# Convolution, two quantised stages and a dense layer in one kernel: another order in front, the bias row spread by TensorE, the second dense half catching up from four steps behind to two

## The chip, the cores and the metric

One core of a Trainium2 chip. The metric is the device time of one execution in microseconds, here the median of three runs. The profile is of one further execution; its times count from the first instruction.

## What is computed

x has shape (64, 64, 1024). The reference, cut to what matters:

```python
out = lax.conv_general_dilated(x, weight, padding=[(4, 4)], feature_group_count=4)   # 9 taps
out = out + einsum('nd,od->no', cond, c_weight)[:, :, None] + fside[None, :, None]
# _fake_quant(v, bits, axis): scale = max|v| / (2**(bits-1) - 1); round(v / scale) * scale
xq = _fake_quant(out, bits=8, axis=-1)
kq = _fake_quant(kernel, bits=8, axis=0)
y = einsum('bsd,df->bsf', xq, kq) + _fake_quant(bias, bits=16, axis=-1)
return x + _fake_quant(y, bits=8, axis=-1)
```

## The kernel before

The 64 x 64 rows of 1024 are cut into 32 tiles of 128 rows (8 samples, one of 4 groups). Each tile goes through five stages, spread over the engines, and the loops of all engines run over steps k = 0, 1, ...:

- ScalarE rounds x of tile k + 2 to a high part (`round_x`, L265), GpSimd subtracts to get the low part (`split`, L218).
- TensorE convolves tile k: two matmuls with the context (L386) and twelve with the taps (L396), in 512 columns each.
- VectorE takes the column maxima (`column_max`, L564, L572), TensorE spreads them over the rows (`spread_max`, L407), VectorE makes the scales (`levels`, L579 to L590) and rounds one half of the tile to integers (L594), ScalarE the other (`round_levels`, L304). One step later TensorE turns these levels (`turn_levels`, L416) and ScalarE copies them to SBUF as bf16 (`take_levels`, L295).
- TensorE multiplies with the kernel, 8 matmuls of 128x512 (`dense`, L427) for each half of the 1024 outputs: the first half of tile k - 2 and the second half of tile k - 4 in step k (`LAG = (2, 4)`). `dense_ps` has one bank of 512 columns for each half. So `dense(t, h)` waits until `biased{h}` of tile t - 1 is signalled: VectorE has multiplied by the scales (`scale_half`, L550) and added the bias into `y` (`add_bias`, L559).
- VectorE takes the maximum of the row of y (`out_scale`, L604 to L611) for tile k - 5 (`TAIL`), ScalarE converts it to integers and back (`quantise`, L312, L315), GpSimd adds x (`add_x`, L227), and a DMA stores it. The last tile goes in halves (`quantise_last` L323, `add_x_last` L618).

The order of each engine is written out by hand, in one loop per engine; an engine does its instructions in this order, and waits stand ahead of the instruction that needs them. All transfers of x and out are issued by SyncE.

In steps 0 to 4 the kernel matrix is prepared between the tiles: four loads of 1 MB (`load_k`), maxima and scales (`k_levels`, L523 to L534), conversion to integers by VectorE or for two of the eight blocks by ScalarE (`k_round`, L270), turning by TensorE (`k_turn`, L440, L449), copies by ScalarE (`k_take`, L277, L279). The banks of `dense_ps` serve for it. The bias is loaded to all 128 partitions (512 KB, L169), VectorE makes its scale in step 1 (`bias_scale`, L540 to L546), ScalarE its levels in step 2 (`bias_levels`, L285, L288).

Of the kernel before, what the change touches and what calls it, by code (L numbers as in the profile page):

```python
# [28 lines left out]
LAG = (2, 4)  # L29
TAIL = LAG[1] + 1  # L30
XWIN, XSPLIT, LEVELS, YRING, ORING, RSRING = 4, 3, 6, 5, 5, 8
# [8 lines left out]
def build(nc, xw, xr, wt, cond_t, cw_t, cond_bias, ker, bias, out):  # L40
    with ExitStack() as ctx:
# [6 lines left out]
        def sem(name):  # L48
# [26 lines left out]
        b_row = sb("b_row", [P, F], F32)  # L75
        b_stat = sb("b_stat", [P, 4], F32)
        b_int = sb("b_int", [P, F], I16)
# [13 lines left out]
        y_max = sb("y_max", [P, 2], F32)  # L91
        y_scale = sb("y_scale", [P, 2], F32)
# [18 lines left out]
            "b_rounded", "b_made",  # L111
# [3 lines left out]
            "y_max_made", "y_scale_made", "y_inv_made", "y_rounded", "y_dequantised", "o_made", "last_rounded", "last_made")}  # L115
# [15 lines left out]
        def there(t):  # L131
            return 0 <= t < TILES

# [15 lines left out]
        def _(sp):  # L149
# [37 lines left out]

            for k in range(1, TILES + TAIL + 1):
                if XWIN <= k + XWIN - 1 < TILES:
                    load_xwin(k + XWIN - 1)  # L190
                if there(k - TAIL + 2):
                    load_x(k - TAIL + 2)
                if 0 <= k - TAIL - 1 < LAST:
                    store(k - TAIL - 1)
# [6 lines left out]
        def _(pool):  # L201
# [32 lines left out]
            for k in range(TILES + TAIL):  # L234
                if there(k + 2):
                    split(k + 2)
                if 0 <= k - TAIL < LAST:
                    add_x(k - TAIL)

        @block.scalar  # L240
        def _(act):
            act.dma_start(condt[:], cond_t).then_inc(s["cond_in"], 16)
            act.dma_start(cwt[:], cw_t).then_inc(s["cond_in"], 16)
            act.dma_start(cbias[:], cond_bias.unsqueeze(0)).then_inc(s["cond_in"], 16)
            act.wait_ge(s["ones_made"], 1)
# [37 lines left out]
            def bias_levels():  # L283
# [4 lines left out]
                act.activation(bq[:], b_int[:], ACT.Copy, scale=b_stat[:, 1:2]  # L288
                               ).then_inc(s["b_made"], 1)
# [36 lines left out]
            round_x(0)  # L326
            k_round(1)
            k_take(0)
            k_take(1)
            round_x(1)  # L330
            for k in range(TILES + TAIL - 1):
                if k == 2:
# [4 lines left out]
                    bias_levels()  # L337
                elif k == 3:
                    k_take(7)
                    k_take(8)  # L340
                    take_levels(2)
# [8 lines left out]
                if k == 0:  # L350
                    k_round(3)
                    k_take(2)
                    k_take(3)
                    k_take(4)
                if there(k - TAIL):
                    quantise(k - TAIL)
# [5 lines left out]
        def _(pe):  # L362
# [48 lines left out]
            def turn_levels(t):  # L411
                wait(pe, "a_rounded_dve", t + 1)
                wait(pe, "a_rounded", t + 1)
                wait(pe, "a_made", t)
                for j in range(NS):
# [47 lines left out]
            for k in range(TILES + LAG[1]):  # L463
# [6 lines left out]
                if k == 1:  # L470
                    k_turns(2, 4)
                if k == 3:
                    k_turns(7, 8)
                if k in (2, 3, TILES):
                    dense(k - LAG[0], 0)
                    if k == TILES:
                        dense(k - LAG[1], 1)
                    turn_levels(k - 1)
                    if k == 2:
                        k_turns(5, 6)  # L480
                    if there(k):
                        spread_max(k)
                elif k == 1:
# [194 lines left out]
```

## Time and profile before

| what | value |
|---|---|
| median of 3 runs | 280.97 us (279.25 to 282.17) |
| the profiled execution, own time | 278.56 us |
| its span, first to last instruction | 276.7 us |
| mean granted TensorE clock | 0.986 |
| busy, TensorE / VectorE / ScalarE / GpSimd | 251.1 / 238.8 / 185.2 / 153.8 us |

Busy time is the time in which an engine ran an instruction; the granted clock is the share of TensorE's full clock that it was given. Own time is longer than the span by 1.86 us of start and end.

### The profile page before, as it was taken

What the parts mean: (1) busy time and instruction counts of PE and PEld (TensorE: products, weight loads), DVE (VectorE), ACT (ScalarE), POOL (GpSimd) and SP (SyncE); (2) the same over time, 40 slices, a digit from 0 to 9 for tenths busy, and PEclk for the clock granted to TensorE, in tenths of its full rate; (3) what the DMA queues carried; (4) which work ended last, traced back from release to release, by engine and by line L of the source; (5) the groups of instructions that cost most, each with busy time, mean ns of one, the idle gap of its engine ahead of it and who ended that gap; (6) DMA issues with size and microseconds to landing.
All of it is one profiled execution on the core that took longest, in us unless ns stands there. A gap on an engine that the chain in (4) does not pass through costs nothing.

```text
span 276.7 us, 4240 instructions
## 1 busy us (share of the span) xinstructions
PE 251.1 (91%) x1372; PEld 163.5 (59%) x1372; DVE 238.8 (86%) x509; ACT 185.2 (67%) x278; POOL 153.8 (56%) x71
## 2 busy tenths in 40 slices
PE   7866769999999999999999999999999999997540
PEld 3555557666666666666666666666666666663210
DVE  1799964799999999999999999999999989999984
ACT  6257586477777777777777777777777767564762
POOL 2533333356666666666666666666666666533453
PEclk9979999999999999999999999999999999999996
DMA  6997322406666565566666766666666663333355
GB/s 253 416 408 301 123 84 103 153 0 227 223 203 212 211 202 212 203 217 217 209 204 210 230 228 228 228 227 226 219 203 197 218 218 117 144 142 139 107 220 219
DMA packets 15799, 56.04 MB, mean 203 GB/s; under 512 B 1954, under 2 KB 1954, under 8 KB 15778
## 3 DMA queue, kind: packets, MB, share of 16 engines
q1 hardware_dynamic: 15488, 55.71, 56.8%
q8 instruction: 11, 0.18, 0.3%
q10 hardware_dynamic: 290, 0.07, 0.1%
q14 instruction: 10, 0.08, 0.1%
HBM read 38.99 MB, written 16.78 MB: 202 GB/s over the span
## 4 chain that ended last, share of the span: by engine, by line
PE 81%; DVE 8%; ACT 4%; DMA 3%; issue 2%; SPq 0%; DVEq 0%
PE dense_ps L427 36%; PE conv_ps L396 31%; PE turn_ps L416 5%; PE conv_ps L386 5%; DMA k_raw<-ffn_kernel 3%; DVE dense_ps L550 2%; DVE y L559 2%; DVE y_max L604 2%; ACT kq L279 2%; PE small_ps L407 2%; PE dense_ps L449 1%; DVE k_max L523 1%; ACT a_int L304 1%; PE dense_ps L440 1%; ACT x_hi L265 1%
## 5 line engine op out<-in xcount | busy, mean ns | idle before, releaser
L427 PE MATMUL dense_ps<-kq,a_t 128*128 128x512 bf16 x512 | 120.6, 379 | 6.1 <-DVE y L559 5.0
L218 POOL TENSOR_TENSOR x_lo<-xwin,x_hi 128x1032 fp32r<-128x1032 f32 x32 | 76.6, 2393 | 80.8 <-ACT x_hi L265 80.8
L227 POOL TENSOR_TENSOR o_sb<-y,o_sb 128x1024 f32<-128x1024 f32 x31 | 73.9, 2384 | 32.8 <-ACT y L315 32.7
L427 PEld LDWEIGHTS dense_ps<-kq,a_t 128*128 128x128 bf16 x512 | 48.9, 101 | 53.7 <-issue 6.7
L295 ACT CAST a_t<-turn_ps 128x1024 bf16<-128x1024 int16 x32 | 32.4, 1012 | 48.5 <-PE turn_ps L416 48.5
L564 DVE TENSOR_REDUCE small_ps<-conv_ps 128x8 f32<-128x1024 f32 x32 | 39.4, 1232 | 13.8 <-PE conv_ps L396 13.5
L550 DVE SCALAR_TENSOR_TENSOR dense_ps<-dense_ps,row_scale,k_scale_b 128x512 f32<-128x512 f32 x64 | 47.7, 745 | 3.6 <-PE dense_ps L427 3.6
L312 ACT ACTIVATE y_int<-y,y_inv 128x1024 int16<-128x1024 f32 x31 | 35.6, 1148 | 22.3 <-DVE y_inv L611 22.1
L559 DVE TENSOR_TENSOR y<-dense_ps,bq 128x512 f32<-128x512 f32 x64 | 43.9, 685 | 2.8 <-ACT bq L288 1.6
L604 DVE TENSOR_REDUCE y_max<-y 128x1 f32<-128x1024 f32 x32 | 38.7, 1210 | 0.7 <-issue 0.2
L304 ACT ACTIVATE a_int<-conv_ps,inv 128x128 int16<-128x128 f32 x128 | 36.0, 363 | 1.1 <-DVE inv L590 1.1
L315 ACT ACTIVATE y<-y_int,y_scale 128x1024 f32<-128x1024 int16 x31 | 35.7, 1153 | 1.0
L396 PE MATMUL conv_ps<-x_hi,w_hi 128*128 128x512 f32 x128 | 36.2, 405 | 0.0
L265 ACT CAST x_hi<-xwin 128x1032 fp32r<-128x1032 f32 x32 | 33.8, 1055 | 3.0 <-DMA xwin<-x_windows 3.0
L396 PE MATMUL conv_ps<-x_hi,w_lo 128*128 128x512 f32 x128 | 35.5, 399 | 0.0
L396 PE MATMUL conv_ps<-x_lo,w_hi 128*128 128x512 f32 x128 | 35.2, 397 | 0.0
L396 PEld LDWEIGHTS conv_ps<-x_hi,w_lo 128*128 128x128 f32 x128 | 24.4, 191 | 6.2
L396 PEld LDWEIGHTS conv_ps<-x_lo,w_hi 128*128 128x128 f32 x128 | 24.0, 188 | 6.2 <-POOL x_lo L218 0.2
L396 PEld LDWEIGHTS conv_ps<-x_hi,w_hi 128*128 128x128 f32 x128 | 24.7, 193 | 4.8
L386 PE MATMUL conv_ps<-select,ctx 128*128 128x512 f32 x64 | 25.0, 474 | 1.9 <-ACT x_hi L265 1.6
L594 DVE TENSOR_TENSOR a_int<-conv_ps,inv 128x512 int16<-128x512 f32 x32 | 22.1, 691 | 1.1
L416 PE MATMUL turn_ps<-ident_b,a_int 128*128 128x128 bf16 x256 | 19.8, 220 | 1.6 <-ACT a_int L304 1.6
(55 smaller groups left out, 160.2 us busy)
## 6 DMA issues: line engine op xcount, KB each, us to landing
xwin<-x_windows SPq DMA_DIRECT2D x32, 516.0 KB, 4.8
o_sb<-x_rows SPq DMA_DIRECT2D x32, 512.0 KB, 5.3
out<-o_sb SPq DMA_DIRECT2D x31, 512.0 KB, 2.9
k_raw<-ffn_kernel SPq DMA_DIRECT2D x4, 1024.0 KB, 10.5
w_raw<-taps SPq DMA_DIRECT2D x2, 256.0 KB, 3.2
b_row<-ffn_bias SPq DMA_DIRECT2D x1, 512.0 KB, 15.9
out<-o_sb SPq DMA_DIRECT2D x2, 256.0 KB, 2.7
condt<-cond_t ACTq DMA_DIRECT2D x1, 32.0 KB
```

Of the source, the lines that this page charges most:

```text
L218: pool.tensor_tensor(x_lo[:, at].rearrange("p n b -> p (n b)"), xwin[:, t % XWIN, :], x_hi[:, at].bitcast(F32).rearrange("p n b -> p (n b) ...
L227: pool.tensor_tensor(o_sb[:, at, :], y[:, t % YRING, :], o_sb[:, at, :], ALU.add).then_inc(s["o_made"], 1)
L265: act.copy(x_hi[:, t % XSPLIT].rearrange("p n b -> p (n b)"), xwin[:, t % XWIN, :]).then_inc(s["hi_made"], 1)
L304: ins = act.activation(a_int[:, at, n * BLOCKS:(n + 1) * BLOCKS], conv_cols(at)[:, n, :], ACT.Copy, scale=inv8[:, at, n:n + 1])
L315: act.activation(y[:, t % YRING, :], y_int[:, t % 2], ACT.Copy, scale=y_scale[:, t % 2:t % 2 + 1]).then_inc(s["y_dequantised"], 1)
L386: mm = pe.matmul(conv_ps[:, at, hs, :].rearrange("p (n b) -> p n b", n=NH), ctx2[:, g].rearrange("k q o -> k (q o)"), select[:, ns].unsque ...
L396: mm = pe.matmul(conv_ps[:, at, hs, :].rearrange("p (n b) -> p n b", n=NH), w[:, ch, g].rearrange("p q o -> p (q o)"), x[:, x_at, hs * NH: ...
L427: mm = pe.matmul(dense_ps[:, h, :], a_t[:, t % LEVELS, q].rearrange("b j o -> b (j o)"), kq[:, q, half(h)], start=(q == 0), stop=(q == Q - 1))
L550: dve.scalar_tensor_tensor(out=dense_ps[:, h, :], in0=dense_ps[:, h, :], scalar=row_scale[:, t % RSRING:t % RSRING + 1], in1=k_scale_b[:, ...
L559: dve.tensor_tensor(y[:, t % YRING, half(h)], dense_ps[:, h, :], bq[:, half(h)], ALU.add).then_inc(s[f"biased{h}"], 1)
L564: dve.tensor_reduce(cmax_ps, conv_ps[:, t % 2].rearrange("p h (n b) -> p (h n) b", b=BLOCKS), AX_X, ALU.max, apply_absolute_value=True).th ...
L604: dve.tensor_reduce(y_max[:, at], y[:, t % YRING, :], AX_X, ALU.max, apply_absolute_value=True).then_inc(s["y_max_made"], 1)
```

## The change

Four edits:

1. `LATE, CATCH_UP = 4, (12, 20)`: the second half of tile t is done in step t + 4 for t below 12, t + 3 from 12 on, t + 2 from 20 on (`second_step`). Steps 15 and 22 hold two second halves; the first of these stands ahead of the convolution. A tile's maximum, quantisation and store follow one step after its second half (`outs`), so that steps 16 and 23 hold two. There are 35 steps in place of 37. `o_sb` has 6 buffers in place of 5, and the load of x rows for tile t is issued in SyncE's step t + 1 in place of t + 3.
2. The bias is loaded to one partition (4 KB, by ScalarE's queue), its statistics and levels are made there, and two float32 matmuls with a row of ones (`bias_spread`) put it into the bank of `turn_ps`, from where ScalarE copies the halves (`bias_take`).
3. The order in front: bias statistics first, kernel maxima apart from kernel scales, x of tile 1 and tile 2 loaded one kernel pair earlier, some copies and turns in another order.
4. The maximum of the last tile is taken in halves (`maximum_last`, `scale_last`).

The diff, cut:

```diff
-LAG = (2, 4)
-TAIL = LAG[1] + 1
-XWIN, XSPLIT, LEVELS, YRING, ORING, RSRING = 4, 3, 6, 5, 5, 8
+LAG, LATE, CATCH_UP = 2, 4, (12, 20)
+XWIN, XSPLIT, LEVELS, YRING, ORING, RSRING = 4, 3, 6, 5, 6, 8
+        def second_step(t):
+            return t + LATE - sum(t >= t0 for t0 in CATCH_UP)
+        def seconds(k):
+            return [t for t in range(TILES) if second_step(t) == k]
+        def outs(k):
+            return seconds(k - 1)
+        STEPS = second_step(LAST) + 2
...
             load_k(0)
+            load_xwin(1)
             load_k(1)
-            load_xwin(1)
             load_k(2)
+            load_xwin(2)
             load_k(3)
-            load_xwin(2)
-            sp.dma_start(b_row[:], bias.partition_broadcast(P)).then_inc(s["b_in"], 16)
...
             round_x(0)
+            bias_levels()
+            round_x(1)
             k_round(1)
+            bias_take(0)
             k_take(0)
             k_take(1)
-            round_x(1)
-            for k in range(TILES + TAIL - 1):
-                if k == 2:
+            bias_take(1)
+            for k in range(STEPS - 1):
+                if k == 0:
+                    round_x(2)
+                elif k == 1:
+                    take_levels(0)
+                    k_round(3)
+                    k_take(2)
+                    k_take(3)
+                    k_take(4)
+                    round_x(3)
+                elif k == 2:
                     take_levels(1)
                     k_take(5)
                     k_take(6)
                     round_x(4)
-                    bias_levels()
...
+                for t in outs(k):
+                    quantise(t)
...
+            def bias_spread(h):
+                pe.wait_ge(s["b_row_made"], 1)
+                wait(pe, "b_made", h)
+                pe.matmul(turn_ps[:].rearrange("b j p -> b (j p)").bitcast(F32), ones[0:1, :],
+                          bq_row[:, half(h)], start=True, stop=True).then_inc(s["b_spread"], 1)
...
+                if len(again) == 2:
+                    dense(again[0], 1)
                 if there(k):
                     conv(k)
                 if k == 0:
+                    bias_spread(0)
                     k_turns(0, 1)
+                    bias_spread(1)
+                    spread_max(k)
...
+            bias_scale()
+            k_maxima(0)
             k_levels(0)
...
+                for t in outs(k):
+                    if t != LAST:
+                        out_scale(t)
...
+                if k - LAG == LAST:
+                    maximum_last(0)
+                if again:
+                    scale_half(again[-1], 1)
+                    add_bias(again[-1], 1)
+            maximum_last(1)
+            scale_last()
             add_x_last()
```

TensorE's order from the end of step 14 to the convolution of step 15; `biased1` is the signal that the second half's bank has been read out. Before:

```order
L407 MATMUL small_ps<-col_max,same_b 128x64 [waits col_max_masked]
L427 MATMUL dense_ps<-kq,a_t 128x512 [waits biased1,a_made]
L427 MATMUL dense_ps<-kq,a_t 128x512 x7
L386 MATMUL conv_ps<-select,ctx 128x512 [waits hi_made,a_rounded,a_rounded_dve]
L386 MATMUL conv_ps<-select,ctx 128x512
```

Now:

```order
L432 MATMUL small_ps<-col_max,same_b 128x64 [waits col_max_masked]
L454 MATMUL dense_ps<-kq,a_t 128x512 [waits biased1,a_made]
L454 MATMUL dense_ps<-kq,a_t 128x512 x7
L454 MATMUL dense_ps<-kq,a_t 128x512 [waits biased1,a_made]
L454 MATMUL dense_ps<-kq,a_t 128x512 x7
L411 MATMUL conv_ps<-select,ctx 128x512 [waits hi_made,a_rounded,a_rounded_dve]
L411 MATMUL conv_ps<-select,ctx 128x512
```

A second group of eight with the same wait stands between the last half of step 14 and the convolution; the same holds ahead of step 22.

ScalarE's order from step 15's levels to step 16's: `take_levels`, `round_x`, `quantise`, `round_levels`. Before:

```order
L295 CAST a_t<-turn_ps 128x8x8x16
L265 CAST x_hi<-xwin 128x1032
L312 ACTIVATE y_int<-y,y_inv 128x1024
L315 ACTIVATE y<-y_int,y_scale 128x1024
L304 ACTIVATE a_int<-conv_ps,inv 128x128 x4
```

Now:

```order
L314 CAST a_t<-turn_ps 128x8x8x16
L279 CAST x_hi<-xwin 128x1032
L331 ACTIVATE y_int<-y,y_inv 128x1024
L334 ACTIVATE y<-y_int,y_scale 128x1024
L331 ACTIVATE y_int<-y,y_inv 128x1024
L334 ACTIVATE y<-y_int,y_scale 128x1024
L323 ACTIVATE a_int<-conv_ps,inv 128x128 x4
```

The second pair of conversions stands ahead of the levels (L304 is L323 now); the same holds in step 23.

VectorE's order at the end, from the bias add of tile 31's first half on. Before (a bias add, the last maximum with its scale, and L618 follow):

```order
L559 TENSOR_TENSOR y<-dense_ps,bq 128x512
L550 SCALAR_TENSOR_TENSOR dense_ps<-dense_ps,row_scale,k_scale_b 128x512
L559 TENSOR_TENSOR y<-dense_ps,bq 128x512
L604 TENSOR_REDUCE y_max<-y 128x1
L608 TENSOR_SCALAR y_scale<-y_max 128x1
L611 RECIPROCAL y_inv<-y_scale 128x1
L550 SCALAR_TENSOR_TENSOR dense_ps<-dense_ps,row_scale,k_scale_b 128x512
L559 TENSOR_TENSOR y<-dense_ps,bq 128x512
L604 TENSOR_REDUCE y_max<-y 128x1
L608 TENSOR_SCALAR y_scale<-y_max 128x1
L611 RECIPROCAL y_inv<-y_scale 128x1
L550 SCALAR_TENSOR_TENSOR dense_ps<-dense_ps,row_scale,k_scale_b 128x512
```

Now:

```order
L603 TENSOR_TENSOR y<-dense_ps,bq 128x512
L682 TENSOR_REDUCE last_max<-y 128x1
L594 SCALAR_TENSOR_TENSOR dense_ps<-dense_ps,row_scale,k_scale_b 128x512
L603 TENSOR_TENSOR y<-dense_ps,bq 128x512
L682 TENSOR_REDUCE last_max<-y 128x1
L671 TENSOR_REDUCE y_max<-last_max 128x1
L675 TENSOR_SCALAR y_scale<-y_max 128x1
L678 RECIPROCAL y_inv<-y_scale 128x1
L662 SCALAR_TENSOR_TENSOR o_sb<-y_int,y_scale,o_sb 128x512 x2
```

The scale and bias of other tiles' second halves and two maxima are gone from between, and the last maximum is in two halves and a small third.

## Rows read from the trace of the kernel before

**Rows 1.** The page: busy time (us, share, instructions), and the chain by line (shares of the span)

```profile
PE 251.1 (91%) x1372; PEld 163.5 (59%) x1372; DVE 238.8 (86%) x509; ACT 185.2 (67%) x278; POOL 153.8 (56%) x71
...
PE dense_ps L427 36%; PE conv_ps L396 31%; PE turn_ps L416 5%; PE conv_ps L386 5%; DMA k_raw<-ffn_kernel 3%; DVE dense_ps L550 2%; DVE y L559 2%; DVE y_max L604 2%; ACT kq L279 2%; PE small_ps L407 2%; PE dense_ps L449 1%; DVE k_max L523 1%
```

**Rows 2.** Stretches: busy us and instructions by engine, granted clock, DMA share, GB/s

```profile
100.00:150.00 50.00, 50.00 (x270) 32.90 (x268) 46.18 (x105) 37.03 (x56) 32.03 (x15) 1.00 0.64 222
```

**Rows 3.** Timeline, TensorE, steps 30 and 31 (start us, duration us, engine, line)

```profile
235.34 0.78 PE L386 MATMUL conv_ps<-select,ctx 128*128 128x512 f32 x2
...
241.13 1.89 PE L427 MATMUL dense_ps<-kq,a_t 128*128 128x512 bf16 x8
...
242.67 0.78 PE L386 MATMUL conv_ps<-select,ctx 128*128 128x512 f32 x2
```

**Rows 4.** Timeline, the end: VectorE and ScalarE

```profile
260.13 0.69 DVE L559 TENSOR_TENSOR y<-dense_ps,bq 128x512 f32<-128x512 f32 x1
...
269.53 1.22 DVE L604 TENSOR_REDUCE y_max<-y 128x1 f32<-128x1024 f32 x1
...
271.17 1.33 ACT L323 ACTIVATE y_int<-y,y_inv 128x512 int16<-128x512 f32 x2 [1.22 <-DVE y_inv L611]
```

**Rows 5.** Timeline, step 31: the second half, and VectorE after it

```profile
248.47 1.89 PE L427 MATMUL dense_ps<-kq,a_t 128*128 128x512 bf16 x8
...
251.18 0.68 DVE L559 TENSOR_TENSOR y<-dense_ps,bq 128x512 f32<-128x512 f32 x1
...
251.78 0.75 DVE L550 SCALAR_TENSOR_TENSOR dense_ps<-dense_ps,row_scale,k_scale_b 128x512 f32<-128x512 f32 x1
...
252.00 3.61 PE L427 MATMUL dense_ps<-kq,a_t 128*128 128x512 bf16 x16 [1.64 <-DVE y L559]
...
252.56 0.69 DVE L559 TENSOR_TENSOR y<-dense_ps,bq 128x512 f32<-128x512 f32 x1
```

**Rows 6.** Timeline, step 31: ScalarE's pair and rounding, TensorE's turn

```profile
242.01 1.15 ACT L312 ACTIVATE y_int<-y,y_inv 128x1024 int16<-128x1024 f32 x1 [1.56 <-DVE y_inv L611]
...
243.20 1.15 ACT L315 ACTIVATE y<-y_int,y_scale 128x1024 f32<-128x1024 int16 x1
...
244.25 1.12 ACT L304 ACTIVATE a_int<-conv_ps,inv 128x128 int16<-128x128 f32 x4
...
246.12 0.62 PE L416 MATMUL turn_ps<-ident_b,a_int 128*128 128x128 bf16 x8
```

**Rows 7.** Stretches of 3.4 us: TensorE busy, clock

```profile
12.80:16.20 3.40, 1.50 (x18) 1.19 (x18) 3.33 (x4) 3.08 (x4) 0.00 (x0) 1.00 1.03 423
...
16.20:19.60 3.40, 3.15 (x7) 2.49 (x8) 3.30 (x4) 0.45 (x2) 2.38 (x1) 0.51 1.02 397
...
262.00:265.40 3.40, 1.89 (x8) 0.71 (x8) 2.83 (x6) 1.30 (x2) 2.23 (x1) 1.00 0.82 293
```

**Rows 8.** Timeline, the front

```profile
6.21 1.98 PE L365 MATMUL dense_ps<-ident 128*128 128x512 f32 x4
...
7.22 0.69 DVE L512 TENSOR_TENSOR ctx<-small_ps,ctx_r 64x512 fp32r<-64x512 f32 x1
...
9.33 2.29 DVE L523 TENSOR_REDUCE k_max<-k_raw 128x2 f32<-128x2048 f32 x1 [1.42 <-DMA k_raw<-ffn_kernel]
...
16.45 1.22 PE L386 MATMUL conv_ps<-select,ctx 128*128 128x512 f32 x2 [1.63 <-ACT x_hi L265]
...
19.35 1.06 ACT L265 CAST x_hi<-xwin 128x1032 fp32r<-128x1032 f32 x1 [2.95 <-DMA xwin<-x_windows]
...
26.41 0.68 PE L386 MATMUL conv_ps<-select,ctx 128*128 128x512 f32 x2
...
36.64 1.15 ACT L285 ACTIVATE b_int<-b_row,b_stat 128x1024 int16<-128x1024 f32 x1
...
44.68 0.68 PE L386 MATMUL conv_ps<-select,ctx 128*128 128x512 f32 x2
```

**Rows 9.** Groups of 0 to 45 us: copies of turned kernel blocks

```profile
L279 ACT CAST kq<-dense_ps 128x1024 bf16<-128x1024 int16 x8 | 7.9, 1016 | 2.2 <-PE dense_ps L449 2.2
```

More of the change, by code:

```diff
@@ L186, in store_last @@
                                  ).then_inc(stored[LAST % ORING], 16)
-            for k in range(1, TILES + TAIL + 1):
+            for k in range(1, STEPS + 1):
                 if XWIN <= k + XWIN - 1 < TILES:
                     load_xwin(k + XWIN - 1)
[L191 to L194, printed above, removed]
+                if there(k - 1):
+                    load_x(k - 1)
+                for t in outs(k - 1):
+                    if t != LAST:
+                        store(t)
             store_last()
@@ L233, in _ @@
                 split(t)
[L234 removed]
+            for k in range(STEPS):
                 if there(k + 2):
                     split(k + 2)
[L237 to L238 removed]
+                for t in outs(k):
+                    if t != LAST:
+                        add_x(t)
         @block.scalar
@@ L287, in bias_levels, with bias_take @@
                 act.wait_ge(s["b_rounded"], 1)
-                act.activation(bq[:], b_int[:], ACT.Copy, scale=b_stat[:, 1:2]
-                               ).then_inc(s["b_made"], 1)
+                act.activation(bq_row[:], b_int[:], ACT.Copy, scale=b_stat[:, 1:2]
+                               ).then_inc(s["b_row_made"], 1)
+            def bias_take(h):
+                act.wait_ge(s["b_spread"], h + 1)
+                act.copy(bq[:, half(h)], turn_ps[:].rearrange("b j p -> b (j p)").bitcast(F32)
+                         ).then_inc(s["b_made"], 1)
             def take_levels(t):
@@ L461, in k_turns @@
                     k_turn(user)
-            for k in range(TILES + LAG[1]):
+            for k in range(STEPS - 1):
+                again = seconds(k)
                 if k == 4:
                     k_turn(9)
+                if len(again) == 2:
+                    dense(again[0], 1)
                 if there(k):
@@ L622, in add_x_last, with scale_last, maximum_last @@
                                              ).then_inc(s["last_made"], 1)
-            k_levels(0)
-            for k in range(TILES + TAIL):
+            def scale_last():
+                at = slice(LAST % 2, LAST % 2 + 1)
+                dve.wait_ge(s["last_max"], 2)
+                dve.tensor_reduce(y_max[:, at], last_max[:], AX_X, ALU.max
+                                  ).then_inc(s["y_max_made"], 1)
+                dve.wait_ge(s["y_max_made"], LAST + 1)
+                wait(dve, "y_dequantised", LAST - 1)
+                dve.tensor_scalar(y_scale[:, at], y_max[:, at], 1.0 / 127, TINY, ALU.mult,
+                                  ALU.max).then_inc(s["y_scale_made"], 1)
+                dve.wait_ge(s["y_scale_made"], LAST + 1)
+                dve.reciprocal(y_inv[:, at], y_scale[:, at]).then_inc(s["y_inv_made"], 1)
+            def maximum_last(h):
+                wait(dve, f"biased{h}", LAST + 1)
+                dve.tensor_reduce(last_max[:, h:h + 1], y[:, LAST % YRING, half(h)], AX_X, ALU.max,
+                                  apply_absolute_value=True).then_inc(s["last_max"], 1)
+            bias_scale()
+            k_maxima(0)
+            k_levels(0)
+            for k in range(STEPS):
+                again = seconds(k)
+                if len(again) == 2:
+                    scale_half(again[0], 1)
+                    add_bias(again[0], 1)
                 if there(k):
```

95 lines of the change are left out of this document (47 added, 48 removed).

## The prediction

> **What bounds the kernel now.** I read the page first: the shares of busy time, then the chain that ended last. TensorE is busy 91% of the span, and in the chain its dense matmuls (L427, 36%) and its convolution matmuls (L396, 31%) are the two large pieces [rows 1]. Then the stretches: between 100 and 150 us TensorE is busy all of the time, VectorE 46.2 of 50 us, ScalarE 37.0, GpSimd 32.0, with the clock at its full level and the DMA engines at 0.64 [rows 2]. So nothing but TensorE's own work sets the time in the middle. Then the timeline, one step: the convolution of step 30 starts at 235.34 and that of step 31 at 242.67, so a step is 7.33 us [rows 3]. The chain shows the same pieces from about 52 us on; what lies before is a front of about 45 us in which the engines wait for each other, and what follows the last convolution (242.67) is a tail of 34.0 us to the end of the span, in which VectorE is the chain. The change touches all three stretches, so the sum has a term for each.
>
> **The tail: it gets shorter.** In the old kernel four second halves (tiles 28 to 31) were left when the convolutions ended; now two are, and there are 35 steps in place of 37. I follow VectorE's queue, since it is late there. Up to the bias add of tile 31's first half the rows of both kernels are the same in kind and number: three maxima, the same first halves, and second halves 29 and 30 where the old kernel had 27 and 28 at these places. So this add still ends at 260.13 + 0.69 = 260.82 [rows 4]. What follows in the new kernel: half a maximum, about 0.62 (half of 1.22 for the whole); scale, 0.75, and bias, 0.69 [rows 5], of tile 31's second half, whose matmuls stand directly behind those of the first half on TensorE and are done by then; the other half maximum, 0.62; a maximum over two numbers, a scale and a reciprocal, about 0.2 each (scale and reciprocal took the 0.42 from 270.75, the old maximum's end, to 271.17). With gaps of 0.05 that is 3.4 us, so the last inverse is ready at about 264.3, where the old one let ScalarE start at 271.17 [rows 4]. What stands behind (5.5 us: two rounds, two adds, two stores) is unchanged. The tail gives 6.9 us. Bounds: the old kernel's four late VectorE groups hold two maxima with their scales (1.6 each) and two scale and bias pairs (1.5 each), 6.2 us of work, to which splitting the last maximum adds 0.3 to 0.7; 6.2 is the low end, 7.6 (if the last stores, no longer side by side with tile 30's, land sooner) the high one. I take 6.9.
>
> **The two catch-up steps: dense.** Tiles 11 and 12 both fall due in step 15, tiles 19 and 20 in step 22. In each of these steps one more second half stands in the middle, where TensorE has no room, ahead of the convolution. Its own 8 matmuls push the next convolution by 1.54 us: old step 30's second half began 1.54 us ahead of the next convolution [rows 3]. But it also waits. There is one PSUM bank for second halves, and the second half of tile 11 may only start when tile 10's has been scaled and had its bias added. Tile 10's is the last thing TensorE did in step 14. How late VectorE is with that can be read in step 31: TensorE started the second half at 248.47 and would be ready for the next work at 250.0 (242.67 + 7.33), VectorE is still in its first half's bias add at 251.18, scales the second half at 251.78 and ends its bias at 252.56 + 0.69 = 253.25 [rows 5]. In the old order a convolution of 3.4 us hid this. Now nothing stands between: the in-order queue holds the convolution, too. With the 0.14 us that passed between 251.86 (end of the first half's bias) and TensorE's start at 252.00, the extra half starts at 253.39, that is 3.39 us after the queue came to it, and the convolution 1.54 later: 4.93 us per catch-up, 9.9 for two. Who waits: VectorE (column maximum of step 15) and by it the whole step; nobody had work in hand that would bring it back, since the step after it is again full for TensorE. Low bound: 1.54 each (no wait), 3.1; high: 1.89 for an undisturbed half with its end and 3.4, so 10.6. I take 9.9.
>
> **The two catch-up steps: quantisation.** One step later (16 and 23) both tiles leave at once. ScalarE stands before a second pair of conversions (y to integers and back, 1.15 + 1.15) ahead of the rounding of the step's levels, and TensorE's turn of these levels stands right behind the next convolution. The row of step 31: the pair starts at 242.01, released by the inverse; the levels are rounded from 244.25 and 1.12 us on, ended at 245.37; TensorE turns them at 246.12 [rows 6]. So 0.75 us are in hand. The second pair with its small gaps is 2.34 us; the second maximum on VectorE (1.6) is done earlier, as it ends 1.6 after the first and the first pair takes 2.34. The levels end at 247.7, plus 0.1: TensorE waits 1.68 us. Two times, 3.4. Bounds: 0 (if the 1.56 us that ScalarE waits ahead of the pair [rows 6] could be used, which the order of its queue doesn't allow) and 4.7. I take 3.4.
>
> **The clock.** The profile shows one fall in the front: over 12.8 to 16.2 us TensorE was busy 1.50 of 3.40, and then the granted clock was 0.51 for 16.2 to 19.6, the 1.2 GHz level; that convolution ran from 16.45 to 21.46 in place of 3.5 us, 1.5 lost. With 1.89 of 3.40 busy (262.0 to 265.4) it stayed at 2.4 GHz [rows 7]. The stall of a catch-up leaves TensorE idle some 3.0 us, after full work. That is between the two rows: each stall costs 0 or 1.5; I take one fall of two, 1.5 us, and keep 0 to 3.0.
> The Trainium skill (TensorE: Matmul & The Clock Gate, section HAM oscillation — how this bites in real kernels) says that long waits between bursts bring the clock down each time, so that every burst starts cold. The one fall of this trace agrees; by that rule both stalls would pay, 3.0 in place of 1.5.
>
> **The front.** The old first convolutions start at 16.45 (step 1), 26.41 (step 2) and 44.68 (step 4) [rows 8]. I lay the new order out with the old durations (a copy of a kernel block 1.02 [rows 9], a cast of x 1.06, a scaled conversion 1.15). Bias statistics (1.2 + 0.4, like the maximum over 1024 in [rows 4]) now stand before the first kernel maximum, which started at 9.33 when its load landed; the operations ahead of it end at 7.9 [rows 8], some 0.2 later for one more DMA issue on ScalarE. So the maximum moves to 9.75. ScalarE: bias rounding, twice 1.15, to 12.1; x of tile 1 to 13.2; kernel block 1 to 14.35; first bias half, about 0.6 for 512 numbers by the 1.02 for 1024, to 15.0. TensorE's second spread is behind that: I price it at 1.0 by the four float32 matmul records of 128x512 that took 1.98 us for two such matmuls [rows 8]. It ends at 16.0, the maximum's spread at 16.3, and the convolution of step 1 starts there: nothing gained, 2 us of new TensorE work hidden in its old idle time. But TensorE was then busy 2.9 of 3.4 us, so I expect no fall of the clock and this convolution ends at 19.8, not 21.46. Behind it ScalarE: levels 21.45, kernel block 3 22.65, copy 23.65, TensorE 24.9 and step 2 at 25.1. Tile 2's x no longer keeps ScalarE (2.95 us, [rows 8]): its load stands ahead of a kernel pair. Step 3 starts at 33.55; there the old 2.3 us of bias conversion (from 36.64) are gone from ScalarE. Its last kernel copies set step 4: 37.0 end of the convolution, first half to 39.3, turn 39.8, levels 40.9, copy 41.9, scale turn 0.95: 42.95 in place of 44.68. The front gives 1.7. Bounds: a gain of 3.5 (1.5 for the clock and 2 for bias and load) and a loss of 0.5 (the clock falls as before, the late maximum comes through).
> Loads of x rows are now issued two steps earlier and a sixth buffer is there; the DMA engines at 0.64 in the middle cover both. If that cover went, the adds on GpSimd would be late, with 18 us of 50 free.
>
> **Sum** against the profiled execution (span 276.7, own time 278.56): -6.9 + 9.9 + 3.4 + 1.5 - 1.7 = +6.2. Span 282.9, own time 284.8. The median of the three runs shown is 280.97, 2.4 above that execution, so the time to expect is 280.97 + 6.2 = 287.1, say 287. About 1% (2.8 us) is what a measurement of this kernel can tell from no change.
>
> **Rivals.**
> First, the catch-up is cheap: the extra half costs its own 1.54 us only, twice, because the bank is free when TensorE comes to it, and the second pair of conversions hides. Then -1.7 + 3.1 - 6.9 = -5.5, 275.5 us. It decides if bias adds end less than 1.2 us after the second half's matmuls were issued; rows 5 show 3.4 us too many, and no step of the middle that I read was another. For it speaks only that VectorE has 3.8 us of 50 free [rows 2]. Chance 0.11.
> Second, the waits are there but the front gives its 3.5, and the clock doesn't fall, and the conversions cost 1 us each time only: -3.5 + 9.9 + 2.0 - 6.9 = +1.5, 282.5 us, within 1%. Chance 0.10.
> Third, the clock falls at every stall: 287.1 + 1.5 = 288.6. The front's fall speaks for it, the level kept in the tail's idle stretches [rows 7] against it. Chance 0.22. This is what the rule of the skill named above would make of it.
> Fourth, the front doesn't do what is meant: bias first on three engines makes the kernel's first blocks late and the clock falls there as before, +0.5 in place of -1.7: 289.3. Chance 0.07.
> My forecast, 287, has 0.50.
>
> **How the numbers follow.** Slower by over 1% (above 283.8): 0.50 + 0.22 + 0.07 = 0.79. Within 1%: 0.10. Faster by over 1%: 0.11. The range for 8 in 10 reaches from 282.0 (the second rival) to 290.0 (the fourth, with a little of spread among runs); it leaves the first rival out. The forecast's own range is 284.5 to 289.5: front 1.8 either way, clock 1.5 either way.
>
> **What the new profile would show.** If right: in the middle, at about 120 and 175 us, two rows of dense matmuls that follow on each other with an idle time of about 3 us before the second, released by the bias add; one step behind each, a turn that waits some 1.7 us for ScalarE's rounding; the period elsewhere 7.33 unchanged; the last convolution some 13 us later than 242.67 (11.5 to 14.5); from it to the end of the span 27 us in place of 34. Step 4's convolution starts near 43 us. What would make it wrong: dense rows back to back at the catch-ups (first rival), a granted clock of 0.5 behind both stalls (third), or convolutions of steps 1 to 4 no earlier than before (fourth).

## The result, and the profile after

The changed kernel takes 291.98 us (median of 4 runs, 290.61 to 293.77) against 281.29 before: ratio 1.0408, 95% interval 1.0331 to 1.0484. That is 11 us slower; 6.2 were forecast. The medians hold every execution, while the ratios and intervals leave out those that ran over 1.5% longer than the fastest of their kernel. The profiled execution has an own time of 293.01 us; its span of 291.3 us is 14.6 above the span before. The medians lie only 10.7 apart, because the profiled execution of before (278.56) was 2.7 below its median and this one is 1.0 above.

The page of the changed kernel (its dense matmuls are L454 now); it answers to [rows 1]:

```profile
span 291.3 us, 4253 instructions
...
PE 261.3 (90%) x1376; PEld 167.5 (58%) x1376; DVE 241.9 (83%) x511; ACT 185.8 (64%) x280; POOL 153.8 (53%) x71
...
PEclk9979979999999999997999999969999999999996
...
PE dense_ps L454 33%; PE conv_ps L421 30%; PE conv_ps L411 5%; PE turn_ps L443 4%; DVE dense_ps L594 3%; PE dense_ps L390 3%; DVE y L603 2%; DVE y_max L648 2%; DVE small_ps L608 2%; PE small_ps L432 2%; DVE k_int L578 1%; PE dense_ps L467 1
```

The clock dips four times before the end (each digit is a fortieth of the span, 7.3 us): twice in the front, in the slices from 14.6 and from 36.4 us, then at about 131 us and at about 190 us. Before, there was one such dip. Where the time went is read from the starts of the convolutions (L411), all from the timelines of the two profiled executions; a step without disturbance is 7.33 us, two are 14.7:

| stretch | before | after | difference |
|---|---|---|---|
| to step 4 | 44.68 | 48.15 | +3.5 |
| steps 14 to 16 | 14.7 | 21.26 (121.44 to 142.70) | +6.6 |
| steps 17 to 18, and 24 to 25 | 7.33 each | 8.90 each | +3.1 |
| steps 21 to 23 | 14.7 | 22.65 (180.95 to 203.60) | +8.0 |
| last convolution to the end | 34.0 | 27.45 (263.83 to 291.28) | -6.6 |

The sum is +14.6. The first catch-up in the timeline (start, duration; VectorE L603 is the bias add, which frees the bank; 155.06 is the turn of step 17). It answers to [rows 5]:

```profile
127.25 1.89 PE L454 MATMUL dense_ps<-kq,a_t 128*128 128x512 bf16 x8
...
131.34 0.69 DVE L603 TENSOR_TENSOR y<-dense_ps,bq 128x512 f32<-128x512 f32 x1
...
132.18 2.86 PE L454 MATMUL dense_ps<-kq,a_t 128*128 128x512 bf16 x8 [3.04 <-DVE y L603]
...
134.48 1.42 PE L411 MATMUL conv_ps<-select,ctx 128*128 128x512 f32 x2
...
155.06 0.61 PE L443 MATMUL turn_ps<-ident_b,a_int 128*128 128x128 bf16 x8 [1.41 <-issue]
```

TensorE's last half of step 14 begins at 127.25, tile 10's bias ends at 132.03, the extra half starts at 132.18 after 3.04 us idle, and takes 2.86 in place of 1.89. Two steps behind each catch-up the turn waits: 1.41 us before 155.06, put down to nothing by the profile; ScalarE's rounding of these levels ended at 154.97. The stretches show the clock and answer to [rows 7]. Their columns are the length, busy time and instructions of TensorE, of its weight loads, of VectorE, ScalarE and GpSimd, then the granted clock, the DMA share and GB/s:

```profile
13.60:17.00 3.40, 3.40 (x23) 1.78 (x23) 3.37 (x3) 2.83 (x5) 1.94 (x1) 0.98 1.03 422
...
17.00:20.40 3.40, 3.40 (x9) 2.63 (x9) 3.26 (x10) 2.48 (x7) 1.88 (x1) 0.52 1.02 418
...
129.20:132.60 3.40, 0.42 (x2) 0.22 (x3) 2.77 (x5) 2.25 (x6) 2.83 (x2) 1.00 0.53 191
...
132.60:136.00 3.40, 3.40 (x10) 1.97 (x9) 0.89 (x2) 0.00 (x0) 0.27 (x1) 0.55 0.69 219
...
187.00:190.40 3.40, 1.63 (x8) 0.55 (x6) 3.05 (x12) 2.75 (x6) 2.78 (x2) 1.00 0.96 327
...
190.40:193.80 3.40, 1.91 (x5) 0.73 (x6) 1.31 (x2) 0.58 (x3) 1.98 (x1) 0.58 0.20 82
...
193.80:197.20 3.40, 3.40 (x9) 2.18 (x8) 1.45 (x2) 0.00 (x0) 0.00 (x0) 0.50 1.00 319
```

Behind both stalls the clock is at the 1.2 GHz level (0.55, 0.58, 0.50), behind the second for two stretches. The tail answers to [rows 4]: half a maximum takes 0.69, and the inverse is ready 21.6 us after the last convolution's start where it was 28.5.

```profile
263.83 0.78 PE L411 MATMUL conv_ps<-select,ctx 128*128 128x512 f32 x2
...
282.03 0.69 DVE L682 TENSOR_REDUCE last_max<-y 128x1 f32<-128x512 f32 x1
...
284.15 0.69 DVE L682 TENSOR_REDUCE last_max<-y 128x1 f32<-128x512 f32 x1
...
284.87 0.15 DVE L671 TENSOR_REDUCE y_max<-last_max 128x1 f32<-128x2 f32 x1
...
285.44 1.33 ACT L342 ACTIVATE y_int<-y,y_inv 128x512 int16<-128x512 f32 x2 [2.46 <-DVE y_inv L678]
```

The front is where the profile shows most of what the forecast missed. VectorE's scale (L570) and conversions (L578) of kernel pairs:

```profile
18.77 2.69 DVE L578 TENSOR_SCALAR k_int<-k_raw,k_inv 128x1024 int16<-128x1024 f32 x1
...
28.37 3.35 DVE L578 TENSOR_SCALAR k_int<-k_raw,k_inv 128x1024 int16<-128x1024 f32 x2
...
37.19 2.06 DVE L570 TENSOR_SCALAR k_scale<-k_max 128x2 f32<-128x2 f32 x1
```

GpSimd's subtraction (L230) at the same time:

```profile
18.52 2.39 POOL L230 TENSOR_TENSOR x_lo<-xwin,x_hi 128x1032 fp32r<-128x1032 f32 x1 [2.98 <-ACT x_hi L279]
...
28.11 2.40 POOL L230 TENSOR_TENSOR x_lo<-xwin,x_hi 128x1032 fp32r<-128x1032 f32 x1 [7.20 <-ACT x_hi L279]
...
36.85 2.38 POOL L230 TENSOR_TENSOR x_lo<-xwin,x_hi 128x1032 fp32r<-128x1032 f32 x1 [6.34 <-ACT x_hi L279]
```

One conversion takes 0.75 us, two 1.42, the scale 0.17. Each of these three is longer by about 1.9, as if it did its work only when GpSimd's row was all but through: 37.19 + 2.06 = 39.25, GpSimd 36.85 + 2.38 = 39.23. The other two end 0.55 us (a row of 0.75) and 1.21 us (a row of 1.42) behind GpSimd's, so all three end 0.15 to 0.21 us sooner than if they had started at its end. TensorE then waits for the conversion behind the third:

```profile
40.38 0.68 PE L476 MATMUL dense_ps<-ident_b,k_int 128*128 128x128 bf16 x8 [2.29 <-DVE k_int L578]
...
41.64 3.13 PE L454 MATMUL dense_ps<-kq,a_t 128*128 128x512 bf16 x8 [0.58 <-DVE y L603]
...
48.15 0.68 PE L411 MATMUL conv_ps<-select,ctx 128*128 128x512 f32 x2
```

Behind this wait of 2.29 us the clock falls, the second dip in the front, and the dense half at 41.64 takes 3.13 us in place of 1.89:

```profile
40.80:44.20 3.40, 2.82 (x11) 0.95 (x9) 2.06 (x4) 1.01 (x1) 0.00 (x0) 0.50 0.72 278
```

### The profile page after: what moved, and what is told of

It reads as the page before. It is cut to its first block, busy times and chain, and to the rows that moved or that the text cites. A ratio compares the mean times of both kernels' runs of the same rounds, so it can differ in the third digit from the quotient of the medians.

```text
span 291.3 us, 4253 instructions
## 1 busy us (share of the span) xinstructions
PE 261.3 (90%) x1376; PEld 167.5 (58%) x1376; DVE 241.9 (83%) x511; ACT 185.8 (64%) x280; POOL 153.8 (53%) x71
## 4 chain that ended last, share of the span: by engine, by line
PE 79%; DVE 14%; issue 3%; ACT 2%; DVEq 0%; POOL 0%; ACTq 0%; POOLq 0%
PE dense_ps L454 33%; PE conv_ps L421 30%; PE conv_ps L411 5%; PE turn_ps L443 4%; DVE dense_ps L594 3%; PE dense_ps L390 3%; DVE y L603 2%; DVE y_max L648 2%; DVE small_ps L608 2%; PE small_ps L432 2%; DVE k_int L578 1%; PE dense_ps L467 1%; DVE k_max L564 1%; PE turn_ps L489 1%; DVE k_scale L570 1%
## 5 line engine op out<-in xcount | busy, mean ns | idle before, releaser
L454 PE MATMUL dense_ps<-kq,a_t 128*128 128x512 bf16 x512 | 124.5, 388 | 9.6 <-DVE y L603 8.5
L230 POOL TENSOR_TENSOR x_lo<-xwin,x_hi 128x1032 fp32r<-128x1032 f32 x32 | 76.7, 2397 | 98.5 <-ACT x_hi L279 98.4
L454 PEld LDWEIGHTS dense_ps<-kq,a_t 128*128 128x128 bf16 x512 | 49.6, 102 | 59.8 <-issue 14.5
L331 ACT ACTIVATE y_int<-y,y_inv 128x1024 int16<-128x1024 f32 x31 | 35.6, 1147 | 17.5 <-DVE y_inv L655 17.2
L603 DVE TENSOR_TENSOR y<-dense_ps,bq 128x512 f32<-128x512 f32 x64 | 44.0, 687 | 1.2
L648 DVE TENSOR_REDUCE y_max<-y 128x1 f32<-128x1024 f32 x31 | 37.5, 1210 | 0.2
L421 PE MATMUL conv_ps<-x_hi,w_hi 128*128 128x512 f32 x128 | 37.2, 415 | 0.0
L323 ACT ACTIVATE a_int<-conv_ps,inv 128x128 int16<-128x128 f32 x128 | 36.0, 363 | 1.1 <-DVE inv L634 1.1
L334 ACT ACTIVATE y<-y_int,y_scale 128x1024 f32<-128x1024 int16 x31 | 35.7, 1153 | 1.0
L421 PEld LDWEIGHTS conv_ps<-x_hi,w_hi 128*128 128x128 f32 x128 | 25.7, 201 | 5.3
L411 PE MATMUL conv_ps<-select,ctx 128*128 128x512 f32 x64 | 26.9, 504 | 0.0
L443 PE MATMUL turn_ps<-ident_b,a_int 128*128 128x128 bf16 x256 | 19.8, 220 | 2.8 <-issue 2.8
```

The source lines that it names most:

```text
L230: pool.tensor_tensor(x_lo[:, at].rearrange("p n b -> p (n b)"), xwin[:, t % XWIN, :], x_hi[:, at].bitcast(F32).rearrange("p n b -> p (n b) ...
L323: ins = act.activation(a_int[:, at, n * BLOCKS:(n + 1) * BLOCKS], conv_cols(at)[:, n, :], ACT.Copy, scale=inv8[:, at, n:n + 1])
L331: act.activation(y_int[:, t % 2], y[:, t % YRING, :], ACT.Copy, scale=y_inv[:, t % 2:t % 2 + 1]).then_inc(s["y_rounded"], 1)
L334: act.activation(y[:, t % YRING, :], y_int[:, t % 2], ACT.Copy, scale=y_scale[:, t % 2:t % 2 + 1]).then_inc(s["y_dequantised"], 1)
L411: mm = pe.matmul(conv_ps[:, at, hs, :].rearrange("p (n b) -> p n b", n=NH), ctx2[:, g].rearrange("k q o -> k (q o)"), select[:, ns].unsque ...
L421: mm = pe.matmul(conv_ps[:, at, hs, :].rearrange("p (n b) -> p n b", n=NH), w[:, ch, g].rearrange("p q o -> p (q o)"), x[:, x_at, hs * NH: ...
```

## The experiments

Each median stands with its ratio to before, measured beside it (medians of 280.9 to 281.5), and the interval of the ratio. An expectation names a theory and a rival, each with its number.

**No catch-up.** `CATCH_UP = (99, 99)`.

> The changed kernel without its catch-up: all second halves four steps behind (37 steps); new front, bias by TensorE and the last maximum in halves are kept. Theory (the new front itself loses time, because VectorE's scale and conversion of kernel blocks now run into GpSimd's subtraction and are held): the convolution of step 4 starts near 48 us as in the changed kernel, and the time is 3 us over before, 284.3. Rival (the front gains what I forecast and all of the loss is the catch-up's): step 4 near 43 us, 279.

282.8 us, ratio 1.0084 (1.0034 to 1.0134); step 4 starts at 48.21. So without the catch-up 2 of the 11 us are left, and the rest is the catch-up's. These 2 are not all the front's: from the last convolution (246.19) to the end of the span (281.9) this kernel takes 35.7 us, where before took 34.0. By the medians the new front costs 0.2 us, by the ratio 0.7, and it doesn't gain the 1.7 of the forecast. The 48.21 stand against one execution of before, whose time of 278.56 is near the low end of its runs.

**Catch-up alone, on the old front.**

> The kernel before with the catch-up in steps 15 and 22, the last maximum in halves, the earlier x row loads and the sixth buffer; front and bias as before. Theory (each catch-up costs a stall of 3.0 us, a clock fall and a late turn, together some 16 to 18 us, and the tail gives 6.6): 289.5, between 287.5 and 292. Rival (the catch-up costs its eight matmuls only): 277.

289.54 us, 1.0271 (1.0204 to 1.0337), the theory's number. Its price was a little high: in the profile the two catch-ups with their late turns cost 14.8 us (steps 14 to 16 are 6.6 longer, 21 to 23 5.1, and twice 1.57), not 16 to 18. The clock fell behind one of the two stalls. And here, in the old order of the front, step 4 starts late too:

```profile
48.66 0.68 PE L399 MATMUL conv_ps<-select,ctx 128*128 128x512 f32 x2
```

That is 4.0 us behind the profile of before, with one held scale as there (17.71 for 2.32 us), but a clock of 0.50 at 17 to 23 and again at 44 to 46 us, where before had it at 16.2 to 19.6 alone. So +3.5 at step 4, read from two single executions, doesn't show what the new order costs. Whether the earlier x row loads, which this kernel also has, take part in it wasn't tested.

**Extra half behind the convolution.**

```diff
-                if len(again) == 2:
-                    dense(again[0], 1)
                 if there(k):
                     conv(k)
+                if len(again) == 2:
+                    dense(again[0], 1)
```

On VectorE the column maximum likewise moves ahead of the extra half's scale and bias.

> The changed kernel with the extra second half of steps 15 and 22 placed behind the convolution (VectorE: behind the column maximum) in place of ahead of it. Theory (the stall is the wait for the one bank of second halves, hidden by a convolution): no idle stretch of 3 us on TensorE at the catch-ups, no clock fall there, each catch-up step longer by 1.7 to 2.3 us; 282, between 280.5 and 284. Rival (VectorE has no room for a second scale and bias in a step, so that the wait only moves): 288 or more.

282.2 us, 1.0047 (1.0009 to 1.0085). The stall is gone and with it both falls; TensorE at step 15, the step's last rows:

```profile
134.77 1.89 PE L454 MATMUL dense_ps<-kq,a_t 128*128 128x512 bf16 x8
...
136.66 1.89 PE L454 MATMUL dense_ps<-kq,a_t 128*128 128x512 bf16 x8
...
138.20 0.78 PE L411 MATMUL conv_ps<-select,ctx 128*128 128x512 f32 x2
```

The step holds three dense halves; the extra one comes first, at 132.58, behind the convolution. The step is 9.05 us (129.15 to 138.20), 1.72 over 7.33, the second 9.21. The wait for the bank was the stall, and a convolution hides it.

**GpSimd waits for VectorE's conversions.**

```diff
             def split(t):
                 wait(pool, "hi_made", t + 1)
+                if 2 <= t <= 4:
+                    pool.wait_ge(s["k_rounded_dve"], 2 * (t - 1))
```

> The changed kernel in which GpSimd's subtraction for tiles 2, 3 and 4 waits until VectorE has made its conversions of kernel pairs 1, 2 and 3. Theory (VectorE's scale and conversion can't run beside GpSimd's subtraction): the rows of 2.69, 3.35 and 2.06 us become 0.75, 1.42 and 0.17, step 4 starts 2 to 5 us earlier, 288. Rival (VectorE is slowed there by something else, the DMA traffic or its own order): these rows stay as long as they were and the time at 292 or more.

284.04 us, 1.0088 (1.0048 to 1.0127), 8 below the changed kernel. The three VectorE rows, and GpSimd's first two subtractions after them:

```profile
18.59 0.75 DVE L580 TENSOR_SCALAR k_int<-k_raw,k_inv 128x1024 int16<-128x1024 f32 x1
...
28.20 1.42 DVE L580 TENSOR_SCALAR k_int<-k_raw,k_inv 128x1024 int16<-128x1024 f32 x2
...
35.38 0.16 DVE L572 TENSOR_SCALAR k_scale<-k_max 128x2 f32<-128x2 f32 x1
```

```profile
19.49 2.41 POOL L232 TENSOR_TENSOR x_lo<-xwin,x_hi 128x1032 fp32r<-128x1032 f32 x1 [4.01 <-DVE k_int L580]
...
29.75 2.37 POOL L232 TENSOR_TENSOR x_lo<-xwin,x_hi 128x1032 fp32r<-128x1032 f32 x1 [7.84 <-DVE k_int L580]
```

0.75, 1.42 and 0.16 us, with nothing changed for VectorE but when GpSimd runs. Step 4 starts at 43.49, 4.7 earlier. Adding waits made it faster. The first two held rows had hardly reached TensorE (steps 2 and 3 start at 26.27 and 34.41 here, 26.43 and 34.58 there). But they had made VectorE late, and the third came on top. Now TensorE has no wait of 2.29 us ahead of step 4, the clock holds there, and of the 4.7 us 1.2 are the dense half that took 3.13:

```profile
38.23 1.89 PE L456 MATMUL dense_ps<-kq,a_t 128*128 128x512 bf16 x8
```

The other 3 us of the median are put down to the clock behind the stalls: in this profile neither brought it down, and then the two catch-ups cost 4.94 and 5.13 us (116.76 to 129.03, and 174.62 to 187.08, less 7.33).

**Stall filled with matmuls.** 13 matmuls of 128x512 ahead of the extra half, whose product nobody uses.

> The changed kernel with 13 matmuls of 128x512 (their product goes to the bank of the turned levels, which is free there, and is used by nobody) ahead of the extra second half in steps 15 and 22, in the time in which TensorE waits. Theory (the stall's idle time makes the clock fall, and the fall costs a further 1.6 to 2.9 us each): the waits of 3.0 us become filled, the granted clock stays at 1.0 behind them, the steps from 14 to 16 take 20 to 20.3 us in place of 21.3; 288.5, between 287 and 290. Rival (a cold clock behind the stall costs nothing that matters, or it falls whatever TensorE does there): 292.

287.9 us, 1.0234 (1.0185 to 1.0284), 4 below the changed kernel. The clock stays at 1.0 behind both stalls, steps 14 to 15 take 12.28 us (126.42 to 138.70) and the next 7.32 (its profiled execution, 293.5 us, is a long one: step 4 starts at 53.14, with four held rows in place of three and a low clock for longer; it is read for these steps alone). So the two falls are worth about 4 us of the median, and what TensorE does in the wait decides over them.

**Both mends.**

> The changed kernel with both edits: the extra second half behind the convolution, and GpSimd's subtraction of tiles 2 to 4 behind VectorE's kernel conversions. Theory (the two losses are independent): 282.2 minus 4.7 = 277.5, faster than before by 1%. Rival (pool_waits gained mostly by its luck with the clock at the stalls): 280 or more.

279.48 us, 0.9866 (0.9804 to 0.9928): about 1% faster than before. By this ratio, which leaves out three of the six runs, the time is 277.4, as the theory had it; the median of all six is 2 us above. Single runs went from 275.4 to 282.3, with mean clocks from 0.988 to 0.973. At least part of the spread is the front's: in the profiled execution (280.66) the clock was low for two stretches there, and a row was held that these waits don't cover, the first conversion beside tile 1's subtraction:

```profile
12.97 2.86 DVE L580 TENSOR_SCALAR k_int<-k_raw,k_inv 128x1024 int16<-128x1024 f32 x1
...
12.91 2.38 POOL L232 TENSOR_TENSOR x_lo<-xwin,x_hi 128x1032 fp32r<-128x1032 f32 x1 [2.15 <-ACT x_hi L281]
```

In the changed kernel's profile the same conversion began at 12.55, ahead of the subtraction at 12.98, and took 0.75: which row is held differs from one execution to another.

**The second pair behind the rounding, too.**

```diff
-                for t in outs(k):
+                for t in outs(k)[:1]:
                     quantise(t)
                 if there(k):
                     round_levels(k)
+                for t in outs(k)[1:]:
+                    quantise(t)
```

On VectorE the second `out_scale` stands behind `levels` in the same way.

> As the one with both edits, and in steps 16 and 23 the second of the two maxima stands behind the levels on VectorE, and the second pair of conversions behind the rounding on ScalarE. Theory (the turn waits 1.4 us for the rounding, and VectorE is then short by 0.5 to 0.8 us in two steps): steps 17 to 18 and 24 to 25 lose 0.7 us in place of 1.57; 275.8 to 276.5. Rival (VectorE's queue is full, so that the second maximum's 1.6 us come back whole): the same as the one with both edits.

275.42 us, 0.9789 (0.9745 to 0.9834). Steps 17 and 24 lose 0.73 us (they take 8.06) in place of 1.57. Its profiled execution took 273.57 us without any fall of the clock before the end:

```profile
span 271.8 us, 4232 instructions
...
PE 250.4 (92%) x1354; PEld 162.6 (60%) x1376; DVE 236.7 (87%) x511; ACT 185.7 (68%) x280; POOL 153.6 (57%) x71
...
PEclk9999999999999999999999999999999999999996
```

**Conversions directly behind their maximum**, undoing that one part of the new order; catch-up as changed.

> The changed kernel with VectorE's scale, inverse and conversions of a kernel pair again directly behind the pair's maximum (ahead of the tile's levels), no other edit. Theory (only the split of maximum and conversion brought them beside GpSimd's subtraction): at least two of the three long rows (2.69, 3.35, 2.06 us) are short, step 4 starts 2 to 4 us earlier than 48.15; 288 to 290. Rival (levels late by the conversions, 1.1 to 1.9 us a step, take it back): 292.

283.57 us, 1.0104 (1.0065 to 1.0143), better than expected: all rows are short (0.76, 1.42 and 1.42), and step 4 starts at 41.71, 3.0 earlier than in the kernel before. VectorE comes to them at 16.66, 23.06 and 31.75, GpSimd to its subtractions at 18.04, 26.15 and 34.90. The clock fell nowhere in this profile. It is the fastest of 12 executions, though (282.05 us, mean clock 0.989); the slowest took 290.5 at 0.965, with the same stalls in the program.

**This with the other two mends** (extra half behind the convolution, second pair behind the rounding).

> The changed kernel with the kernel pair's conversions directly behind their maximum, the extra second half behind the convolution and the second pair of conversions behind the rounding; GpSimd has no extra waits. Theory (the two ways to keep VectorE's conversions and GpSimd's subtraction apart are worth the same): 275.4, within 1 us of the one that used GpSimd's waits, and over 1.5% faster than before. Rival (the conversions ahead of the levels cost the front something that the waits didn't): 277 or more.

275.47 us, 0.9821 (0.9774 to 0.9868). The two ways to keep the engines apart are worth the same.

**The same front without catch-up.**

> The changed kernel with the kernel pair's conversions directly behind their maximum and without any catch-up (all second halves four steps behind). Theory (a catch-up without stall costs 1.8 for its matmuls and 0.7 for the second maximum, twice 2.5, and the tail gives 6.6): 1 to 2 us slower than the version that has all three mends, 276.5 to 277.5, and still faster than before by 3 to 4 us, by the front alone. Rival (the catch-up is worth nothing even when mended, since the tail's gain is given back in the middle): 275.4.

280.04 us, 0.9988 (0.9956 to 1.0019): the theory missed by 3 us. The catch-up, once mended, is worth 4.6. Against the first experiment, which differs only in where the conversions stand, this is 2.8 us less (280.04 for 282.8), the price of the held rows and of the clock that fell behind them, without a catch-up. The reason for the miss is in its tail: 35.6 us from the last convolution (242.36 to 278.0), 1.6 more than before. With four late halves the halved maximum isn't a gain: the last inverse comes 28.7 us after that start, before 28.5. What more of the tail is behind the inverse, 1.4 us, wasn't taken apart further; one row there, the last two adds, took 1.99 in place of 1.59. In this profile the clock fell for two stretches in the front, and step 4 starts at 44.37, where before had 44.68.

**The old bias in the mended kernel.**

> The version with all three mends (conversions directly behind the maximum, extra second half behind the convolution, second pair behind the rounding), but with the bias as before: 512 KB to all partitions, statistics in step 1, levels by ScalarE in step 2, no spreading matmuls. Theory (the bias on one row takes 2.3 us of ScalarE out of step 2 and puts them where ScalarE had waited; its two matmuls don't keep the clock up): the old bias costs 1 to 2.5 us, 276.5 to 278. Rival (the early bias only moves the same work, and its 1.2 us maximum and two conversions ahead of the first blocks cost as much): 275.5, or less.

281.63 us, 1.0024 (0.999 to 1.0057). 6 us lost, outside the theory (277 to 278) and the rival (275.5), by a way that neither had named. Two rows fell beside GpSimd again: the first conversion, at 12.39 for 2.64 us, and the scale at 18.79 for 2.34. VectorE came to this conversion when it had before (12.44 in the three mends' profile); it is GpSimd that was early, at 12.08 in place of 12.91, since ScalarE rounded tile 1's x at 10.95 in place of 11.80 with no bias levels ahead of it.

**The old bias, with GpSimd's waits for tiles 1 to 4.**

> The version with the old bias once more, with GpSimd's subtraction of tiles 1 to 4 behind VectorE's conversions of kernel pairs 0 to 3. Theory (most of the old bias's 6 us were two conversions that fell beside GpSimd's subtraction again, 1.9 and 2.2 us too long, because nothing stood ahead of the kernel maxima any more; the bias path itself is worth its 2.3 us of ScalarE in step 2): both rows short, 277 to 278.5. Rival (the bias path itself is worth the 6 us): 281.

277.09 us, 0.9861 (0.982 to 0.9902). So 4.5 of the 6 us go with these two collisions, and the bias path by itself is worth about 1.6, a difference between two kernels whose intervals (0.982 to 0.9902, and 0.9774 to 0.9868) overlap.

## Why the prediction was wrong

The forecast had the sign and missed the size: 287 with a range to 290, measured 292. Its terms, by the profiles:

- *The tail*, -6.9: -6.6 in the profile; the part up to the last inverse gave 6.9 as laid out, what stands behind took 0.3 more. The layout's pieces with their gaps add up to 3.6, not the 3.4 that it used; that the rows took 3.4 is luck.
- *Catch-up, dense*, 4.93 each: 4.94 and 5.13 where the clock held (GpSimd-waits and whole-conversion kernels). Right, by its mechanism.
- *Catch-up, quantisation*, 1.68 each: 1.57 each. Right; moving the pair left 0.73.
- *The clock at the stalls*, one fall of 1.5 in two, is the term that was sized too small: it fell behind both in the changed kernel's profile, and cost 1.6 and 2.9 us, the second over two stretches; filling the stalls gave 4 us of the median. Over the four profiled kernels that have the stall (changed, catch-up alone, GpSimd waits, whole conversions) 3 of 8 stalls brought it down. The third rival had the right idea, and 3.0 for its price was too low. The Trainium skill (TensorE: Matmul & The Clock Gate, section HAM oscillation — how this bites in real kernels) has every burst behind a long wait start cold; here 3 of 8 did.
- *The front*, -1.7, is the step that failed in its mechanism: +3.5 to step 4 in the profile, 0.2 to 0.7 by the medians and ratios, no gain by either. "I lay the new order out with the old durations": the layout was near at step 1 (16.3 forecast, 16.71) and within 1.4 us at steps 2 and 3 (25.1 and 33.55; 26.43 and 34.58), and then 5.2 off at step 4, because a conversion of 0.75 us isn't one beside GpSimd's subtraction. Moving scale and conversions behind `levels` put them there three times; behind the wait that came of it the clock fell once more. With GpSimd made to wait, step 4 starts at 43.49 where 42.95 was forecast. So the new order has a gain, and the held rows ate it.
- *No fall of the clock in the front*, "TensorE was then busy 2.9 of 3.4 us, so I expect no fall of the clock": it was busy 3.40 of 3.40 (13.6 to 17.0) and the clock fell all the same to 0.52, so that step 1's convolution ended at 21.8, where 19.8 was forecast.

How sure the front's number is, the starts of step 4 in all profiles of these fronts tell (us):

| front | step 4 starts at |
|---|---|
| old order (before, catch-up alone) | 44.68, 48.66 |
| new order (changed, no catch-up, half behind, filled) | 48.15, 48.21, 48.52, 53.14 |
| new order with GpSimd's waits (alone, both, with the late pair) | 43.49, 46.68, 41.27 |
| new order, conversions directly behind the maximum (alone, with the mends, without catch-up) | 41.71, 42.73, 44.37 |

One and the same front differs by 2 to 5 us from execution to execution (41.27, 43.49, 46.68). Still, every profile of the changed front is behind every one of the two mended fronts. The old front overlaps with both, so that the profile's +3.5 overstates the loss. In the medians the miss is 4.5 us (10.7 for 6.2). My estimate of its parts: about 2 are the front, which cost up to 0.7 where it was to give 1.7, and about 2.5 the clock at the stalls, 4 in place of 1.5.

The collision could have been read before. The old kernel has it once, in the timeline before:

```profile
16.48 2.38 POOL L218 TENSOR_TENSOR x_lo<-xwin,x_hi 128x1032 fp32r<-128x1032 f32 x1 [5.81 <-ACT x_hi L265]
16.56 2.33 DVE L526 TENSOR_SCALAR k_scale<-k_max 128x2 f32<-128x2 f32 x1
```

I had looked at the mean of the group. The Trainium skill (SBUF — State Buffer, section Who interferes with whom) says that GpSimd and VectorE share a pair of SBUF ports as an exclusive lock, which VectorE's scalar forms can take in their fast mode, but reductions never; the one that comes second waits to the end. The trace agrees in the main: the held rows end 0.15 to 0.21 us sooner than a start at GpSimd's end would have it, and VectorE's kernel maximum (2.25 to 2.29 us in all kernels) is never longer, beside GpSimd neither. By that rule and these rows, step 4 would have been forecast, as an estimate, at 43 us plus up to three times 1.9.

## What to carry to other kernels

A duration from a trace holds for the neighbours it had: when an order moves a VectorE copy or scalar operation, look what GpSimd runs at the new time, and a wait that lets the short one go first can pay (step 4 starts 4.7 us earlier here, and the median is 8 lower, with the clock at the stalls in it). Work that shares one buffer with the instruction just ahead of it belongs behind something long; here moving 8 matmuls behind the convolution gave 10 us. And when a step holds double work, let the second part stand behind what the next engine waits for: with these three mends the change is about 2% faster than the kernel before, in place of 4% slower. And one profile of each kernel isn't enough for a part of it whose clock varies: the same front started step 4 at 41.27, 43.49 and 46.68.

## What the runs showed that I had not expected

The clock fell behind full busy time: at 13.6 to 17.0 us TensorE was busy 3.40 of 3.40, two bias spreads (at 13.37 and 15.41, 1.12 us each) and 16 transposes among it, and the clock then was 0.52; in [rows 7] it stayed at 1.00 behind 1.89 of 3.40. These instructions alone don't decide it: the kernel with whole conversions has them too, was busy 3.68 of 4.00 at 12 to 16 us, and kept 1.00. The wait of 2.3 us ahead of step 4, on the other hand, was followed by a fall in all four profiles that have it (2.29 to 2.30), the old order's wait of 2.21 at that place in one of two, the stalls of 3.0 to 3.3 us in 3 of 8. And an operation on 128x2 numbers, 0.17 us, is held as long as a large one: 2.06. What decides whether the clock falls behind one and the same stall stays open; no run here told.
